# The involution's sums over taps in 32-column blocks, four column groups at a time

## The reference

```python
def _L1_conv_ref(x, W1, b1, W2, b2):
    ...
    wgt = jnp.einsum('bhwc,cd->bhwd', x, W1) + b1
    wgt = jnp.einsum('bhwd,de->bhwe', wgt, W2) + b2
    wgt = wgt.transpose(0, 3, 1, 2).reshape(b, G, 1, kk, h, w)
    ...
    patches = jnp.stack([xp[:, i:i + h, j:j + w, :] for i in range(K) for j in range(K)], axis=3)
    out = patches.reshape(b, h, w, kk * c).transpose(0, 3, 1, 2).reshape(b, G, GC, kk, h, w)
    out = jnp.einsum('bgokhw,bgckhw->bgchw', wgt, out)
```

## Time and profile before

| | |
|---|---|
| median of 3 runs | 2615.26 us (2614.51 to 2618.99) |
| span of the profiled execution | 2612.6 us |
| busy, share of the span: TensorE | 1841.8 us, 70% |
| VectorE | 1736.1 us, 66% |
| ScalarE | 1167.3 us, 45% |
| GpSimd | 1064.7 us, 41% |
| mean granted TensorE clock | 0.846 |

### The profile page before, as it was taken

The page is one execution under the profiler, slowest core; times in us unless marked ns, Lnnn a source line. Parts: engine busy times, 40 slices in busy tenths (PEclk is TensorE's granted clock), DMA queues, the critical chain, the costliest instruction groups (busy, mean ns, idle before and its releaser), DMA issues. The chain is left out here.

```text
span 2612.6 us, 45588 instructions
## 1 busy us (share of the span) xinstructions
PE 1841.8 (70%) x10450; PEld 1310.7 (50%) x10467; DVE 1736.1 (66%) x5126; ACT 1167.3 (45%) x2450; POOL 1064.7 (41%) x993
## 2 busy tenths in 40 slices
PE   1476233399258888299996288919982999929992
PEld 1232133388234344188885144418872544419992
DVE  6998699488757777444443777745657677765664
ACT  2333465277232333155553288804443544416661
POOL 0144133244102434444444216656763045555662
PEclk9777555599679999599998599959996999969996
DMA  2000100121210000122223201113324201113336
GB/s 67 0 1 7 60 23 25 45 62 54 71 66 17 28 26 29 48 67 58 58 58 104 93 12 41 44 47 99 97 72 150 78 28 34 33 55 93 85 89 203
DMA packets 171905, 151.86 MB, mean 58 GB/s; under 512 B 28958, under 2 KB 151590, under 8 KB 171746
## 3 DMA queue, kind: packets, MB, share of 16 engines
q1 hardware_dynamic: 141794, 90.82, 12.5%
q0 software_dynamic: 29952, 59.26, 6.5%
HBM read 83.77 MB, written 68.79 MB: 58 GB/s over the span
## 5 line engine op out<-in xcount | busy, mean ns | idle before, releaser
L1033 POOL DMA_INDIRECT returned<-channel_major x488 | 480.2, 984 | 456.3 <-DVE channel_major L992 323.0
L878 PE MATMUL psum<-channel_major 128*128 128x128 f32 x3360 | 460.6, 277 | 1.1 <-ACT channel_major L925 1.1
L941 ACT ACTIVATE channel_major<-psum,bias_columns 128x128 f32<-128x128 f32 x1104 | 323.1, 367 | 293.3 <-PE psum L878 292.7
L894 PE MATMUL psum<-expert_weights,channel_major 128*128 x2784 | 427.6, 288 | 0.6 <-DVE channel_major L981 0.6
L878 PEld LDWEIGHTS psum<-channel_major 128*128 128x128 f32 x3360 | 420.4, 194 | 1.2 <-issue 1.2
L706 POOL DMA_INDIRECT dispatched<-rows_first_choice,slot x192 | 194.7, 1014 | 547.8 <-DVE rows_second_choice L632 399.2
L894 PEld LDWEIGHTS psum<-expert_weights,channel_major 128*128 128x128 f32 x2784 | 348.9, 191 | 25.1 <-issue 2.0
L706 POOL DMA_INDIRECT dispatched<-rows_second_choice,slot x192 | 196.6, 1024 | 68.6 <-issue 66.8
L992 DVE TENSOR_SCALAR channel_major<-psum,channel_major 128x128 f32<-128x128 f32 x416 | 144.8, 348 | 98.0 <-PE psum L894 93.5
L969 DVE COPY channel_major<-expert_weights 128x512 f32 (+1 forms) x272 | 100.4, 369 | 157.3 <-PE psum L878 147.9
L326 PE MATMUL psum<-identity,rows_first_choice 128*128 128x128 f32 x256 | 42.3, 327 | 195.2 <-DVE rows_first_choice L313 182.6
(11 more groups left out here) (328 smaller groups left out, 3602.0 us busy)
## 6 DMA issues: line engine op xcount, KB each, us to landing
channel_major<-dispatched SPq DMA_DIRECT2D x488, 65.0 KB
expert_weights<-returned SPq DMA_DIRECT2D x12, 1024.0 KB, 10.3
rows_second_choice<-returned SPq DMA_DIRECT2D x8, 1024.0 KB, 10.8
returned<-channel_major POOLq DMA_INDIRECT x488
expert_weights<-in_L_ffn_w SPq DMA_DIRECT2D x3, 2048.0 KB, 9.2
residual<-in_x SPq DMA_DIRECT2D x8, 512.0 KB, 7.2
rows_first_choice<-returned SPq DMA_DIRECT2D x4, 1024.0 KB, 9.0
out<-residual SPq DMA_DIRECT2D x8, 512.0 KB, 6.0
```

Source lines behind the costliest of these rows:

```text
L878: ins = pe.matmul(k.ps[:, PSH + u % 2, j * P:(j + 1) * P], wc[:, u % 2, j * P:(j + 1) * P], xt[:, u % 2, :], start=True, stop=True)
L894: ins = pe.matmul(bank, gs[:, u % HB, j * P:(j + 1) * P], second[:, bass.ds(e, 1), j, :].rearrange("p a c -> p (a c)"), start=(b2 is None ...
L941: ins = act.activation(hs[:, u % HB, cols], k.ps[:, PSH + u % 2, cols], f["act"], bias=bcol[:, bass.ds(e * J + j, 1)])
L1033: pool.indirect_dma_start(out=k.returned[0:N * K, :], out_offset=bass.IndirectOffsetOnAxis(ap=rt[:, u, C:C + 1].bitcast(I32), axis=0), in_ ...
```

## The change

The sums are split by output columns. For each tap, only the groups of 32 output columns are computed into which its rows fall: one group for six taps and two for three taps, 12 matmuls of 32 columns instead of 9 of 128. They are put into three rounds of four (`ROUNDS`), and in each round the four matmuls write to the four groups of 32 partitions of the bank, each from another product or another column group. The taps are computed in another order (`ORDER`), so that the first four products suffice for round 0, the first eight for round 1 and all nine for round 2 (`READY`). The products lie in eight buffers instead of four (`DEEP`), all at the start of the expert weights' tensor; product m waits for the round that read product m - 8 (`LAST`). Because these buffers lie where the expert weights go, SyncE waits for the last sum ahead of `load_weights`.

Round 0 of a half stands behind its seventh kernel pair, rounds 1 and 2 behind the second pair of the next half. `turn_back` moves from behind pair 2 to behind pair 3, `add` on VectorE from product 3 to 4 and `norm` from 5 to 6. The hidden matmul of half 1 now stands ahead of `turn_back`.

```diff
--- before.py
+++ after.py
@@ -1355,6 +1355,11 @@
     GROUPS = i["L1_conv_W2"].shape[1] // TAPS
     GC = C // GROUPS
     PER = 2 * TAPS
+    ORDER = (0, 3, 5, 7, 1, 2, 4, 8, 6)
+    ROUNDS = (((0, 0), (3, 1), (5, 2), (7, 3)), ((1, 0), (2, 1), (4, 2), (8, 3)), ((2, 0), (4, 1), (6, 2), (6, 3)))
+    READY = (4, 8, 9)
+    LAST = [max(r for r, parts in enumerate(ROUNDS) if tap in [t for t, _ in parts]) for tap in ORDER]
+    DEEP = 8
     names = ("inv_loaded", "inv_prep", "inv_bias", "inv_ones", "inv_hidden", "inv_part", "inv_rest", "inv_kernel", "inv_product",
              "inv_sum", "inv_stored")
     s = {n: k.sem(n) for n in names}
@@ -1377,15 +1382,13 @@
         hidden_parts = k.flat(k.rows0)[:, tail].bitcast(BF16).rearrange("p (x a n) -> p x a n", x=2, a=2)
         hid_a, hid_b = hidden_parts[:, 0], hidden_parts[:, 1]
         rest = sb("hidden_rest", [P, BANK])
-        prods = [k.flat(k.rows1)[:, tail][:, 0:BANK], k.flat(k.rows1)[:, tail][:, BANK:2 * BANK]]
+        prods = k.wts[:, 0:DEEP * BANK].rearrange("p (a n) -> p a n", n=BANK)
         used = 2 * FFN[1]["E"] * FFN[1]["F"]
         spans = k.wts[:, used:used + TAPS * C].bitcast(BF16).rearrange("p (x n) -> p x n", x=2)
         span_a, span_b = spans[:, 0], spans[:, 1]
         gather = k.wts[:, used + TAPS * C:used + 2 * TAPS * C].rearrange("p (t c) -> p t c", t=TAPS)
         left = used + 2 * TAPS * C
         mixed_first = k.wts[:, left:left + IMG]
-        prods.append(k.wts[:, left + IMG:left + IMG + BANK])
-        prods.append(sb("last_product", [P, BANK])[:])
         bias_row = k.flat(k.rows1)[0:1, 0:TAPS * C]
 
         def mixed(b):
@@ -1411,6 +1414,8 @@
             sp.dma_start(b2row[:], i["L1_conv_b2"].rearrange("(a c) -> a c", a=1)).then_inc(s["inv_loaded"].h, 16)
             sp.wait_ge(*when("inv_loaded", loads))
             route.load_gate(sp)
+
+            sp.wait_ge(*when("inv_sum", 3 * 2 * B))
             route.load_weights(sp)
             route.send_pads(sp)
 
@@ -1439,8 +1444,6 @@
             pe.wait_ge(*when("inv_ones", 3))
             pe.wait_ge(*when("inv_prep", PREP))
 
-            LAG = 3
-
             def hidden(b, half):
                 if 2 * b + half:
                     pe.wait_ge(*when("inv_rest", 3 * (2 * b + half) - 2))
@@ -1448,8 +1451,8 @@
                           window(b, half, 1, 1), start=True, stop=True).then_inc(s["inv_hidden"].h, 1)
 
             def kernel_entries(b, n):
-                half, tap = n // TAPS, n % TAPS
-                if tap == 0:
+                half, tap = n // TAPS, ORDER[n % TAPS]
+                if n % TAPS == 0:
                     pe.wait_ge(*when("inv_rest", 3 * (2 * b + half) + 3))
                 if b * PER + n >= 3:
                     pe.wait_ge(*when("inv_product", b * PER + n - 2))
@@ -1458,13 +1461,16 @@
                 pe.matmul(k.ps[:, 1 + n % 3, :], span_b[:, cols], hid_b[:, half, :], start=False,
                           stop=True).then_inc(s["inv_kernel"].h, 1)
 
-            def add_up(b, n):
-                half, tap = n // TAPS, n % TAPS
-                if tap == 0 and b:
-                    pe.wait_ge(*when("inv_stored", 2 * b + half - 1))
-                pe.wait_ge(*when("inv_product", b * PER + n + 1))
-                pe.matmul(k.ps[:, 4 + half, :], gather[:, tap, :], prods[(b * PER + n) % 4], start=(tap == 0),
-                          stop=(tap == TAPS - 1)).then_inc(s["inv_sum"].h, 1)
+            def add_up(h, r):
+
+                if r == 0 and h >= 2:
+                    pe.wait_ge(*when("inv_stored", h - 1))
+                pe.wait_ge(*when("inv_product", h * TAPS + READY[r]))
+                for tap, g in ROUNDS[r]:
+                    cols = slice(32 * g, 32 * g + 32)
+                    ins = pe.matmul(k.ps[cols, 4 + h % 2, :], gather[:, tap, cols],
+                                    prods[:, (h * TAPS + ORDER.index(tap)) % DEEP, :], start=(r == 0), stop=(r == 2))
+                ins.then_inc(s["inv_sum"].h, 1)
 
             hidden(0, 0)
             for b in range(B):
@@ -1474,11 +1480,15 @@
                     if n == 11 and b + 1 < B:
                         hidden(b + 1, 0)
                     kernel_entries(b, n)
-                    if n >= LAG:
-                        add_up(b, n - LAG)
-                    route.tensor_between(pe, b, n, (2, 7, 10, 13))
-                for n in range(PER - LAG, PER):
-                    add_up(b, n)
+                    h = 2 * b + n // TAPS
+                    if n % TAPS == 1 and h:
+                        add_up(h - 1, 1)
+                        add_up(h - 1, 2)
+                    if n % TAPS == 6:
+                        add_up(h, 0)
+                    route.tensor_between(pe, b, n, (3, 7, 10, 13))
+            add_up(2 * B - 1, 1)
+            add_up(2 * B - 1, 2)
             route.finish_tensor(pe)
 
         @block.scalar
@@ -1499,7 +1509,7 @@
                 act.activation(hid_b[2 * RED:3 * RED, half, :], rest[2 * RED:3 * RED, :], ACT.Copy).then_inc(s["inv_part"].h, 1)
 
             def store(b, half):
-                act.wait_ge(*when("inv_sum", b * PER + (half + 1) * TAPS))
+                act.wait_ge(*when("inv_sum", 3 * (2 * b + half + 1)))
                 act.activation(mixed(b)[:, half * BANK:(half + 1) * BANK], k.ps[:, 4 + half, :],
                                ACT.Copy).then_inc(s["inv_stored"].h, 1)
 
@@ -1566,15 +1576,16 @@
             route.reset(dve)
             for b in range(B):
                 for n in range(PER):
-                    half, tap = n // TAPS, n % TAPS
+                    half, tap = n // TAPS, ORDER[n % TAPS]
                     dve.wait_ge(*when("inv_kernel", b * PER + n + 1))
-                    if b * PER + n >= 4:
-                        dve.wait_ge(*when("inv_sum", b * PER + n - 3))
+                    old = b * PER + n - DEEP
+                    if old >= 0:
+                        dve.wait_ge(*when("inv_sum", 3 * (old // TAPS) + LAST[old % TAPS] + 1))
                     dve.scalar_tensor_tensor(
-                        out=prods[(b * PER + n) % 4].rearrange("p (h w) -> p h w", w=WW),
+                        out=prods[:, (b * PER + n) % DEEP, :].rearrange("p (h w) -> p h w", w=WW),
                         in0=k.ps[:, 1 + n % 3, :].rearrange("p (h w) -> p h w", w=WW), scalar=b2[:, tap:tap + 1],
                         in1=window(b, half, tap // 3, tap % 3), op0=ALU.add, op1=ALU.mult).then_inc(s["inv_product"].h, 1)
-                    route.vector_between(dve, b, n, (3, 5, 11, 15))
+                    route.vector_between(dve, b, n, (4, 6, 11, 15))
                     if n in (4, 6):
                         (leave if n == 4 else third)(b, 1)
                     if n in (12, 14) and b + 1 < B:
```

## The result

The changed kernel takes 2634.76 us (2634.61 to 2635.26, 3 runs) where the kernel before takes 2615.26: a ratio of 1.0068, 95% interval 1.005 to 1.0086, 19.5 us slower. The forecast was 2668. The side and the range were right; the loss came out at little more than a third of the forecast's 52.8 us. The time is that of the rival "four groups at once", 2634.

What follows compares the result with a forecast made beforehand. TensorE and VectorE, neither full, were bound by waiting for each other. Seven images (+47.7), image 0 (0), end (+4.1) and load (+1) gave +52.8 us on 2612.6; the median lies 2.7 higher: 2668, range 2603 to 2692.

Steps and rivals of the forecast that it cites:

- four groups at once: Rival: matmuls of all four column groups overlap, a block takes 1.72 us, clock still lost; 2634 us, chance 0.25.
- B: Time of the eight matmuls of rounds 1 and 2 on TensorE, twice per image: 3.87 us, bounds 1.7 and 6.9.
- image 0: The image without a router: product 16 at 781.6 + B against 785.50, taken as 0 for B = 3.87.
- Layout of the stretches: One image on VectorE in four stretches: 32.74 + 2B us at full clock, against 37.66 before.
- stretch 1: VectorE from product 16 to the router's `add`: 5.12 + B us at full clock, against 8.64 before.
- Stretch 2: VectorE from `add` to product 7: 10.67 us, with `leave` starting 0.91 us after `add`.
- Stretch 4: VectorE from product 11 to product 16: 12.43 us, the same rows in the same order.
- The clock: TensorE begins both blocks at 1.2 GHz after idling: 4.0 us lost per image, bounds 0 and 5.5.
- Stretch 3: VectorE from product 7 to product 11: 4.52 + B us at full clock, against 5.89 before.
- faster: Rival: all four column groups overlap and TensorE's clock stays up, 36.2 us per image; 2603 us, chance 0.14.
- End and load: Last block half in low clock, +4.1 us; the later load of the expert weights, +1 us, bounds 0 and 12.
- Order of taps, eight buffers: In the involution, the new order of taps costs nothing; eight buffers spare VectorE no wait.

Runs made afterwards that it cites:

- e8: The changed kernel with all eight matmuls of rounds 1 and 2 in column group 0: 2898.95 us, 1.0311 of the kernel before.
- e2: The changed kernel with the eight matmuls of rounds 1 and 2 sorted by column group: 1.0075 of the kernel before.
- e6: The changed kernel with rounds 1 and 2 behind pairs 13 and 2, hidden matmuls and gate moved too: 0.9975 and 0.9997 of the kernel before.
- e9: The kernel of e6 with `leave` and `third` one product later: 1.004 of the kernel before.
- e10: The kernel of e6 with full-width sums of 128 columns: 1.009 of the kernel before.
- e1: The changed kernel with the sums as nine matmuls of 128 columns again, rounds in their new places: 1.0133 of the kernel before.
- e3: The changed kernel with 54 unused bf16 matmuls per image in TensorE's idle pieces: 1.0051 of the kernel before.

## Why the prediction was right in sign and wrong in size

**The step that failed is B.** The prediction put the block at 9 x 0.43 = 3.87 us, for "only the second half of one can run beside the first half of the next". The block takes 1.85 us, four halves of 0.43 and 0.13 more. The single records come in fours: in the block at 924.95 four halves start within 0.02 us (924.95 to 924.97), four at 925.41 to 925.42, four at 925.84 to 925.85 and the last at 926.27 to 926.28. The weight loads go with them, those of the first eight halves at once, then four and four:

```profile
924.95 0.16 PEld L1471 LDWEIGHTS psum<-expert_weights 128*32 128x32 f32 x8 [0.84 <-DVE expert_weights L1584]
925.41 0.13 PEld L1471 LDWEIGHTS psum<-expert_weights 128*32 128x32 f32 x4 [0.30 <-issue]
925.84 0.13 PEld L1471 LDWEIGHTS psum<-expert_weights 128*32 128x32 f32 x4 [0.30 <-issue]
```

The records don't name the group. But in e8's block at 870.02, with one group, no two halves start closer than 0.43 us, so the four that start together are of four groups. Halves of one group follow each other like those of full width; those of other groups don't wait for them. e2 shows that sorting them by group costs 0.03 us at most, e8 that without the groups the time is all there. The rule of the Trainium skill by which B was 1.7 (TensorE: Matmul & The Clock Gate, Part 3: Packing small matmuls: four column tiles span one matmul plus some nanoseconds) was the right one, for f32 as well: 1.85 for two rounds, four times 0.43 plus 0.13. I weighed its sentence on starting in program order against it, and read an order of starts in the earlier trace rows as a rule about groups that those rows don't contain.

Twice 2.02 us over seven images are 28 of the 33 us by which the forecast missed; image 0 and the end, which rest on B too, are most of the rest. With 1.85 the prediction's own sum is 7 x (32.74 + 3.70 + 4.0 - 37.66) = +19.5, image 0 -2.0, end +2.4, load +1: 2636 us.

**The other terms.**
- *Layout of the stretches.* Full clock, B taken as 1.85: 6.97 for stretch 1, measured 7.10 in image 1. Stretch 2: 10.67, measured 10.69; `leave` idles 1.00 us where 0.91 was said, and no wait for a product in it. Stretch 4: 12.43, measured 12.43. The sequence of work was right.
- *The clock.* Said: 2.2 and 1.8 us per image. Against 6.97 and 6.37 at full clock the measured 9.68 and 8.15 are 2.7 and 1.8. The second held; the first was 0.5 too small: the clock is low from 943.41 until the pair behind the block (948.35, whose matmul takes 0.63 us), longer than the 4.4 us that were taken. Stretch 3 of image 1 has 1.0 us of it. The rival "faster", with a clock that stays up, had the same layout and fell by this term alone; it is also what turns image 1, a draw at 37.60, into 40.95.
- *Image 0* was said to end 2.0 us sooner by B = 1.85; product 16 comes 21.5 us after the first for 22.1, so 0.6. Its block took 3.04 us (772.36 to 775.40): the clock falls in image 0 too, behind 2.0 us without work, and I had counted no loss there.
- *End and load.* The last block takes 3.2 us, 1062.28 to 1065.50; +1.1 us is seen at the experts' start, where the sum, with B as 1.85, held 2.4 + 1.
- *Order of taps, eight buffers.* In the changed kernel no product waits for a sum. With the blocks elsewhere they do (e6, e9, e10), so this holds for this order only.

**Why less work takes longer.** 50 us less of TensorE bought nothing, since most of the 7.7 us of sums per half image had lain between pairs, beside VectorE's products: it is waiting for pairs alone. The change gathers the rest in two blocks ahead of pairs that VectorE waits for, and the emptier engine drops to 1.2 GHz. e1 and e6 take this apart at image 1: in the new places the narrow width is worth 4.5 us per image (42.32 to 37.81), which brings it level with the kernel before; the other places are worth 3.2 more. Of the 18.5 us by which the loop has grown, images 2 to 7 hold all: in them the clock is low in both stretches. How the loss divides can be estimated from stretches with the clock up: 6.95 + 10.69 + 5.89 + 12.43 = 35.96 us for an old image (the first from the kernel before on the second chip), 7.15 + 10.69 + 6.58 + 12.43 = 36.85 for a new one (the first and third from e3). So about 0.9 of the 3.3 us per image is the places, and about 2.4 is that the clock takes 4.1 us where it took 1.7. No run shows this split as a whole time.

**What stays open.** How e6 would do on the first chip wasn't measured, nor a kernel whose clock stays up there. What the idleness without a releaser is, and why it shrinks to nothing when the blocks are long (`add` to product 7 is 10.7 us in every image of e8, 13.5 to 14.9 from image 2 on in the changed kernel on that chip), isn't known.

## What to carry to other kernels

Price a block of small matmuls by its fullest column group, not by its count. Before taking work off an engine, ask who waits behind it: a sum between two pairs may be free, and a block half as long in front of one costs its length. And after thinning TensorE's work, look for the idle pieces of 2 us and more that it leaves, and for what stands right behind them: here it ran at half speed, for some 4 us per image by the estimate above.

## What was not expected of the hardware

- Eight f32 matmuls of 32 x 512 take 1.85 us spread over four column groups, 1.88 with neighbours in the same group, and 6.98 us in one group at full clock (e8).
- Within one group the halves stand 0.43 us apart, as at full width: 32 columns are no faster than 128.
- A load of 10 us at 370 GB/s beside indirect sends left their issue at 1.27 us apart; their landings took up to 6.9 us (3.9 in the kernel before), where 2.3 was the shortest.
- The same kernel takes 2615 us in the runs of the result and 2809 to 2817 on two other chips. Of 187 us between two profiles the loop holds 21. A variant that is 3 us better in one image shows little of it in the sum there.
